# Output projection in half batches of four heads and pairs of query tiles; gates of the expert branch placed by a table

## The chip, the cores and the metric

The kernel runs on one core of a Trainium2 chip. The core has TensorE (matmuls, with weight loads beside them), VectorE, ScalarE, GpSimd and SyncE, which here only issues transfers. Each has its own queue of instructions, worked off in order, and they hand work to each other over semaphores. In the rows PE, PEld, DVE, ACT, POOL and SP stand for TensorE's matmuls, its weight loads, VectorE, ScalarE, GpSimd and SyncE. The metric is the device time of one execution in microseconds (us).

## The reference, cut to what matters

```python
x = L0_attn_x                                # (4, 1024, 256)
xn = _layernorm(x)
# attention: 8 heads of 128, one key and one value for all heads of a batch
q = (xn @ Wq + bq) + pe ; k = (xn @ Wkv + bkv)[..., :128] + pe ; v = ...[..., 128:]
probs = softmax(causal(q k^T / sqrt(128)))
s = concat_over_heads(probs @ v) @ Wo        # (4, 1024, 1024) @ (1024, 256)
# experts: 8 of them, two per token, weighted by the router
f = sum over the token's two experts of gate_e * (relu(xn @ w1_e + b1_e) @ w2_e + b2_e)
out = x + s * silu(f)
```

## The kernel before, in words

Two stages follow each other. Up to about 474 us routing and experts run (`front`); they leave the experts' outputs in DRAM. From then on `attention` runs, and only it is changed.

**Heads and steps.** The four batches have eight heads each, so there are NH = 32 batch-heads, numbered 0 to 31 and called heads here. A head has eight query tiles of 128 rows, done in five groups (`GROUPS`: tile 7; 6 and 0; 5 and 1; 4 and 2; 3). Step k = 5 n + i is group i of head n. Numbers are held as a high and a low half in 16 bits, and each product is three matmuls (`PASSES`).

**A step.** TensorE computes the scores of step k (L1144, L1147 adds the mask) and, one head late, the values of a pair of tiles of head n - 1 (L1167, L1169). VectorE takes row maxima (L1347) from PSUM, ScalarE the exponentials (L1252), VectorE the reciprocals of their sums (L1376), ScalarE the high half of the probabilities (L1282), VectorE the low half (L1383: both of its tensors, `pr` and `ph`, lie in SBUF). SyncE issues a transposing transfer of both halves (L1498), whose result `pT` the values read. The values' result is split into `outs` by ScalarE (L1260) and VectorE (L1389).

**Jobs.** `Jobs` lists one projection of 512 columns for some steps: queries of head n + 2 at i = 0 and 2 of each head, and in heads 4 to 7 of each batch but the last one of keys or values of the next batch at i = 1 (L1101). A query or key job goes TensorE, VectorE (positions, L1356), ScalarE (L1272), VectorE (L1370). The job at i = 0 uses the bank `psJ`, and so does the output projection.

**Output projection before.** `outs` has two buffers of a whole batch. `o_tile(c)` (L1183) multiplies query tile c of a finished batch with `wo` over all eight heads, 24 matmuls of 256 columns into the half bank `psJ[:, 0:D]`. It runs at i = 4 of heads 9 to 31 and once behind the last head, for the TILES = 24 tiles of the first three batches. VectorE multiplies the result by the gate `G` at the start of the next head (`o_gated`, L1410), GpSimd adds `x` (`added`, L1472, 256 columns), SyncE stores and loads 128 KB per tile (L1502, L1507). The last batch's eight tiles are done in `rows_out` (L1194), 192 matmuls of 256 columns in all, into the banks of the scores behind the last head; `closing` (L1443) multiplies them by `G_last` and GpSimd adds `x` (L1487), the last pair VectorE (L1457).

**Gates.** For each of 32 tiles GpSimd fetches the two expert rows of each token (`fetch`, L1466), ScalarE weighs the first (`weigh`, L1290), VectorE adds the second (`whole_f`, L1395), ScalarE takes the tanh (L1301), VectorE forms `G` (`gated`, L1404). Before, one tile is gated in each of heads 1 to 31, at i = 1 to 4, and one behind them: first the last batch's eight, then tiles 0 to 23.

In the loops of all engines i == 0 of the following head comes right behind i == 4; what an engine does there stands first in its step.

## Time and profile before

| | us |
|---|---|
| time, median of three runs (lowest, highest) | 1087.91 (1086.62, 1091.30) |
| the profiled execution: time | 1086.89 |
| its span, first to last instruction | 1085.0 |
| busy: TensorE | 995.2 (92%) |
| busy: VectorE | 859.1 (79%) |
| busy: ScalarE | 644.6 (59%) |
| busy: GpSimd | 324.9 (30%) |

The span is what the profile's clock shows between the first and the last instruction; the time has 1.9 us more around it. Shares are means over stages with different limits, so they are read by stretch. A timeline row gives the start, the duration (of the group, where several like instructions are merged: "x24"), engine, line, operation, and in brackets the idle time of the engine before it with what ended that. A releaser can be misnamed where two events came close together.

### The profile page before, as it was taken

The page shows a single profiled execution, that of the slowest core. Times are in us where ns is not written, and L with a number is a line of the kernel's source. Part 1 is how long each engine was busy: PE and PEld are TensorE (multiplying, and loading weights), DVE is VectorE, ACT ScalarE, POOL GpSimd, SP SyncE. Part 2 cuts the span into 40 slices and gives each one's busy share as a digit, 9 for nine tenths or more (in the row PEclk, how much of TensorE's full clock was granted, in tenths as well). Part 3 has the DMA queues.
Part 4 walks back from the last instruction along what each step waited for, and adds up shares of the span by engine and source line. Part 5 has one row for each costly group of instructions (what it writes and reads, how often), then busy time and mean ns, then how long its engine had stood idle before and what let it go on. Part 6 is the DMA issues. An engine that isn't in the chain of part 4 may idle for free.

```text
span 1085.0 us, 25159 instructions
## 1 busy us (share of the span) xinstructions
PE 995.2 (92%) x8734; PEld 783.7 (72%) x8734; DVE 859.1 (79%) x1543; ACT 644.6 (59%) x1360; POOL 324.9 (30%) x339
## 2 busy tenths in 40 slices
PE   1647999999999999998889889999999999999997
PEld 1536888888888898965656667767677677777776
DVE  6885777666766555569999999998999999999971
ACT  3812333233333333348888888878888888888860
POOL 0005999899994200020011102121112111112111
PEclk9999999999999999999999999999999999999999
DMA  8548776766665312137897888998999879898992
GB/s 281 178 192 182 154 186 172 173 175 178 178 171 157 89 50 55 37 102 147 165 162 141 158 159 177 164 149 153 171 185 178 148 147 170 160 173 160 175 183 90
DMA packets 402810, 168.80 MB, mean 156 GB/s; under 512 B 345562, under 2 KB 393252, under 8 KB 402052
## 3 DMA queue, kind: packets, MB, share of 16 engines
q1 hardware_dynamic: 345632, 127.04, 56.1%
q10 hardware_dynamic: 50580, 22.45, 8.6%
q0 software_dynamic: 6480, 17.70, 6.6%
q8 instruction: 78, 1.28, 0.5%
q14 instruction: 40, 0.33, 0.1%
HBM read 51.66 MB, written 30.67 MB: 76 GB/s over the span
## 4 chain that ended last, share of the span: by engine, by line
PE 35%; DVE 13%; DMA 3%; ACT 3%; issue 2%; SPq 0%; ACTq 0%; DVEq 0%
PE b_psS L1144 10%; PE b_psO L1167 10%; PE b_psJ L1183 5%; PE b_psJ L1101 4%; DVE b_ph L1383 4%; DVE b_nmax L1347 4%; DMA b_pT<-b_ph 3%; PE b_psS L1194 2%; PE b_psS L1101 1%; PE b_psO L1169 1%; DVE b_outs L1389 1%; ACT b_pr L1252 1%; ACT b_ph L1282 1%; DVE b_psJ L1356 1%; PE b_psS L1147 1%
## 5 line engine op out<-in xcount | busy, mean ns | idle before, releaser
L847 PE MATMUL psU<-bxT,w_p 128*128 128x256 f16 (+1 forms) x1920 | 287.9, 263 | 13.3 <-DVE w_p L273 10.4
L922 ACT ACTIVATE h<-psU,bias 128x256 f32<-128x256 f32 (+1 forms) x320 | 124.7, 447 | 284.9 <-PE psU L847 192.8
L856 PE MATMUL psY<-w_p,hp 128*128 x1704 | 272.4, 273 | 1.8 <-DVE hp L944 1.3
L1144 PE MATMUL b_psS<-b_kp,b_Q 128*128 128x512 f16 (+3 forms) x1152 | 218.4, 326 | 0.1
L847 PEld LDWEIGHTS psU<-bxT,w_p 128*128 x1920 | 189.1, 98 | 33.8 <-issue 15.1
L1252 ACT ACTIVATE b_pr<-b_psS,b_nmax 128x1024 f32<-128x1024 f32 (+7 forms) x256 | 186.7, 734 | 42.4 <-DVE b_nmax L1347 22.8
L1167 PE MATMUL b_psO<-b_pT,b_vp 128*128 128x256 f16 x1536 | 188.6, 272 | 18.1 <-issue 8.4
L1383 DVE SCALAR_TENSOR_TENSOR b_ph<-b_pr,b_rrec,b_ph 128x1024 f16<-128x1024 f32 (+7 forms) x256 | 199.1, 809 | 0.0
L1282 ACT ACTIVATE b_ph<-b_pr,b_rrec 128x1024 f16<-128x1024 f32 (+7 forms) x256 | 187.0, 768 | 15.9 <-DVE b_rrec L1376 15.6
L942 DVE CAST hp<-h 128x512 f16<-128x512 f32 (+1 forms) x160 | 88.5, 553 | 134.0 <-ACT h L922 127.1
L1347 DVE TENSOR_REDUCE b_nmax<-b_psS 128x1 f32<-128x1024 f32 (+7 forms) x256 | 182.7, 745 | 9.2 <-PE b_psS L1147 7.3
L856 PEld LDWEIGHTS psY<-w_p,hp 128*128 128x128 f16 x1704 | 166.2, 98 | 22.8 <-issue 2.9
L1167 PEld LDWEIGHTS b_psO<-b_pT,b_vp 128*128 128x128 f16 x1536 | 144.5, 98 | 41.4 <-issue 14.4
L1144 PEld LDWEIGHTS b_psS<-b_kp,b_Q 128*128 128x128 f16 x1152 | 103.0, 98 | 77.2 <-issue 0.6
L1466 POOL DMA_INDIRECT b_yg<-expert_outputs,pos x64 | 68.6, 1071 | 245.0 <-DVE b_f L1395 119.1
L944 DVE TENSOR_TENSOR hp<-h,hp 128x512 f16<-128x512 f32 (+1 forms) x160 | 129.7, 811 | 5.5
L1472 POOL TENSOR_TENSOR b_x_row<-b_G,b_x_row 128x256 f32<-128x256 f32 x24 | 17.4, 726 | 366.9 <-DVE b_G L1410 358.1
L172 POOL DMA_INDIRECT rowx<-xn_split,who x71 | 78.8, 1110 | 99.6 <-DVE who L753 77.2
L1183 PE MATMUL b_psJ<-b_wo,b_outs 128*128 128x256 f16 x576 | 66.9, 273 | 0.3 <-DVE b_Q L1370 0.3
L262 POOL TENSOR_TENSOR w_p<-wstage,w_p 128x512 f16<-128x512 f32 x48 | 64.1, 1336 | 4.1
L1183 PEld LDWEIGHTS b_psJ<-b_wo,b_outs 128*128 128x128 f16 x576 | 55.1, 98 | 7.0 <-DVE b_Q L1370 0.5
L1272 ACT ACTIVATE b_Q<-b_psJ,bias 128x512 f16<-128x512 f32 x59 | 40.5, 687 | 31.3 <-DVE b_psJ L1356 30.6
(181 smaller groups left out, 1029.4 us busy)
## 6 DMA issues: line engine op xcount, KB each, us to landing
wstage<-in_L_ffn_w SPq DMA_DIRECT2D x48, 256.0 KB
expert_rows<-rowx SPq DMA_DIRECT2D x67, 128.0 KB
expert_outputs<-y ACTq DMA_DIRECT2D x31, 256.0 KB
a_x_all<-in_L_attn_x SPq DMA_DIRECT2D x8, 512.0 KB, 9.8
a_w_raw<-in_L_ffn_w SPq DMA_DIRECT2D x4, 1024.0 KB, 6.5
xn_split<-a_xp SPq DMA_DIRECT2D x4, 1024.0 KB, 4.9
xn_turned<-a_xT SPq DMA_DIRECT2D x3, 1024.0 KB, 12.8
b_x_row<-in_L_attn_x SPq DMA_DIRECT2D x24, 128.0 KB, 2.6
```

The costliest lines, as they stand in the source:

```text
L847: mm = eng.matmul(psU[w % U][:, g % 2, 0:tiles * P].rearrange("p (t r) -> p t r", t=tiles), weight(n, a * W1 + c * H + g * P, P), bxT[n % ...
L856: mm = eng.matmul(psY[n % 2][:, t, :], hp[n % 2][:, a, g, t * P:(t + 1) * P], weight(n, 2 * W1 + (2 * g + b) * D, D), start=(g == 0 and k ...
L922: a = eng.activation(h32[w % 4][:, g, 0:rows], psU[w % U][:, g, 0:rows], ACT.Relu, bias=bias[:, ds(e * HT + 2 * q + g, 1)], scale=1.0 / WS)
L942: eng.tensor_copy(hi, full).then_inc(hh_, 1)
L944: eng.tensor_tensor(lo, full, hi, ALU.subtract).then_inc(hl_, 1)
L1144: mm = eng.matmul(dst, Q[n % 3][:, a, u * P:(u + 1) * P], kb[:, c, lo:lo + w], start=(kk == 0), stop=(kk == 2 and not last))
L1167: eng.matmul(both, vb[:, a, j, :], pT[:, at:at + hop + 1:hop, :], start=(j == 0 and kk == 0), stop=False)
L1183: mm = eng.matmul(psJ[:, 0:D], outs[b % many][:, a, h, t * P:(t + 1) * P], wo_p[:, e, h, :], start=(h == 0 and kk == 0), stop=(h == HEADS ...
L1252: a = eng.activation(pr[k % 3][:, o:o + w], psS[BUF[i]][:, :, :].rearrange("p a n -> p (a n)")[:, o:o + w], ACT.Exp, bias=nmax[:, at:at + ...
L1282: a = eng.activation(ph[k % 4][:, 2 * o:2 * o + w], pr[k % 3][:, o:o + w], ACT.Copy, scale=rrec[:, at:at + 1])
L1347: a = eng.tensor_reduce(nmax[:, at:at + 1], psS[BUF[i]][:, :, :].rearrange("p a n -> p (a n)")[:, o:o + w], AX.X, ALU.max, negate=True)
L1383: a = eng.scalar_tensor_tensor(ph[k % 4][:, 2 * o + w:2 * o + 2 * w], pr[k % 3][:, o:o + w], rrec[:, at:at + 1], ph[k % 4][:, 2 * o:2 * o ...
```

## The change

The output projection works on half batches. `outs` is one buffer of a batch. Portion r (`o_pair(r)`, r = 0 to 27) takes four heads (the first or the second half of a batch's eight) and two query tiles: 2 x 4 x 3 = 24 matmuls of 256 columns, into the whole bank `psJ`. It runs at i = 4 of head r + 5, that is of heads 5 to 31, and portion 27 behind the last head. `two_of(r)` gives which half it is and the number g of the pair of tiles.

- First half of the heads (r % 8 below 4): ScalarE copies the bank to `part` (`o_part`), at the start of heads 6 to 9, 14 to 17, 22 to 25, 30, 31 and behind them.
- Second half: VectorE adds the bank to `part` (`o_sum`), at the start of heads 10 to 13, 18 to 21 and 26 to 29; then GpSimd multiplies `part` by `G` (`weighted`) and adds it to `x_rows` (`added`), each 512 columns; SyncE loads and stores pairs of 256 KB.
- Last batch: its first four heads are portions 24 to 27. GpSimd multiplies them by `G_last` and adds them to `x_last` (`added_last`), which is loaded (1 MB) in head 8 and no longer behind the last head. `rows_out` keeps heads 4 to 7: 96 matmuls.
- Gates follow the table `gates`: tiles 0 to 23 in heads 4 to 27, the last eight as a second gate, one step later, in heads 12 to 15 and 20 to 23. Heads 1 to 3 and 28 to 31 have none.
- New waits: ScalarE waits for the experts' stores ahead of its loop, VectorE for four `added_last` ahead of the last head's `o_low`.

```diff
-    seq = list(range(TILES, NT)) + list(range(TILES))
-    turn_of = {c: s for s, c in enumerate(seq)}
+    PART, MORE = HEADS // 2, TILES // 2
+    gates = [(5 * n + 1 + x, c) for n in range(NH) for x, c in enumerate(
+        ([n - PART] if PART <= n < PART + TILES else []) + ([TILES + n % HEADS - PART + n // HEADS * PART - PART]
+                                                            if n % HEADS >= PART and 0 < n // HEADS < 3 else []))]
+    gate_at = dict(gates)
+    turn_of = {c: s for s, (_, c) in enumerate(gates)}
...
-        xr = [sb(f"x_row{i}", [P, D], F32) for i in range(3)]
+        xr = [sb(f"x_rows{i}", [P, 2, D], F32) for i in range(3)]
...
-        Gb = [sb(f"G{i}", [P, D], F32) for i in range(2)]
-        outs = [sb(f"outs{i}", [P, 2, HEADS, T], F16) for i in range(2)]
+        Gp = [sb(f"G{i}", [P, 2, D], F32) for i in range(4)]
+        part = [sb(f"part{i}", [P, 2, D], F32) for i in range(4)]
+        outs = sb("outs", [P, 2, HEADS, T], F16)
...
-        over = Arena(nc, q_at)
-        fin = over.take("b_x_last", [P, QT, D], F32)
...
+        def two_of(r):
+
+            m, p = r // 4, r % 4
+            return m % 2, 4 * (m // 2) + p
+
+        def bank_free(eng, r):
+
+            second, g = two_of(r)
+            eng.wait_ge(ot_ if second else oe_, g + 1)
...
-            def o_tile(c):
...
+            def o_pair(r):
+
+                m, p = r // 4, r % 4
...
-                eng.wait_ge(al_, 2 * HEADS * (b + 1))
-                if c:
-                    eng.wait_ge(ot_, c)
-                for h in range(HEADS):
-                    for kk, (a, e) in enumerate(PASSES):
-                        mm = eng.matmul(psJ[:, 0:D], outs[b % many][:, a, h, t * P:(t + 1) * P], wo_p[:, e, h, :],
-                                        start=(h == 0 and kk == 0), stop=(h == HEADS - 1 and kk == 2))
+                eng.wait_ge(al_, 2 * PART * (m + 1))
+                if r:
+                    bank_free(eng, r - 1)
+                h0 = PART * (m % 2)
+                for x in range(2):
+                    t = 2 * p + x
+                    for h in range(h0, h0 + PART):
+                        for kk, (a, e) in enumerate(PASSES):
+                            mm = eng.matmul(psJ[:, x * D:(x + 1) * D], outs[:, a, h, t * P:(t + 1) * P], wo_p[:, e, h, :],
+                                            start=(x == 0 and h == h0 and kk == 0), stop=(x == 1 and h == h0 + PART - 1 and kk == 2))
                 mm.then_inc(om_, 1)
...
-                        if i == 0 and n >= HEADS + 2:
-                            eng.wait_ge(ot_, n - HEADS - 1)
+                        if i == 0 and n >= PART + 2:
+                            bank_free(eng, n - PART - 2)
...
-                    if i == 4 and n > HEADS:
+                    if i == 4 and n > PART:
                         eng.wait_ge(jl_, jobs.issued(k + 1))
-                        o_tile(n - HEADS - 1)
+                        o_pair(n - PART - 1)
...
-            rows_out(0, 0, HEADS - 2)
-            o_tile(TILES - 1)
+            rows_out(0, PART, HEADS - 2)
+            o_pair(NH - PART - 1)
...
             rows_out(0, HEADS - 2, HEADS - 1)
-            rows_out(3, 0, HEADS - 1)
+            rows_out(3, PART, HEADS - 1)
...
-            rows_out(2, 0, HEADS - 1)
...
-            rows_out(1, 0, HEADS - 1)
+            rows_out(1, PART, HEADS - 1)
...
-                if n >= 2 * HEADS and n % HEADS == 0 and half == 0:
-                    eng.wait_ge(om_, n - HEADS)
+                if n >= HEADS and n % PART == 0 and half == 0:
+                    eng.wait_ge(om_, n - PART)
...
+            def o_part(g):
+                eng.wait_ge(om_, 4 * (2 * (g // 4)) + g % 4 + 1)
+                if g >= 4:
+                    eng.wait_ge(oa_, g - 3)
+                eng.activation(part[g % 4][:, :, :].rearrange("p t d -> p (t d)"), psJ[:, :], ACT.Copy, scale=0.5 / WS).then_inc(oe_, 1)
...
+            for i, o in enumerate(v["y_o"]):
+                eng.wait_ge(o, 16 * len(range(i, NBLK, 3)))
             for k in range(LAST + 2):
                 n, i = k // 5, k % 5
+                if i == 0 and n >= PART + 2 and not two_of(n - PART - 2)[0]:
+                    o_part(two_of(n - PART - 2)[1])
...
-                if k < LAST and n:
-                    if i == 1:
-                        weigh(seq[n - 1])
-                    if i == 3:
-                        tanh(seq[n - 1])
-            weigh(TILES - 1)
-            tanh(TILES - 1)
+                if k in gate_at:
+                    weigh(gate_at[k])
+                if k - 2 in gate_at:
+                    tanh(gate_at[k - 2])
+            o_part(two_of(NH - PART - 1)[1])
...
-                if 2 <= c < TILES:
-                    eng.wait_ge(oa_, c - 1)
-                dst = Gb[c % 2][:, :] if c < TILES else GD[:, c - TILES, :]
+                if 8 <= c < TILES:
+                    eng.wait_ge(oa_, c // 2 - 3)
+                dst = Gp[c // 2 % 4][:, c % 2, :] if c < TILES else GD[:, c - TILES, :]
...
-            def o_gated(c):
-                g = Gb[c % 2][:, :]
-                eng.wait_ge(G_, turn_of[c] + 1)
-                eng.wait_ge(om_, c + 1)
-                eng.scalar_tensor_tensor(g, psJ[:, 0:D], 0.5 / WS, g, ALU.mult, ALU.mult).then_inc(ot_, 1)
+            def o_sum(g):
+                whole = part[g % 4][:, :, :].rearrange("p t d -> p (t d)")
+                eng.wait_ge(oe_, g + 1)
+                eng.wait_ge(om_, 4 * (2 * (g // 4) + 1) + g % 4 + 1)
+                eng.scalar_tensor_tensor(whole, psJ[:, :], 0.5 / WS, whole, ALU.mult, ALU.add).then_inc(ot_, 1)
...
-                if i == 0 and n >= HEADS + 2:
-                    o_gated(n - HEADS - 2)
+                if i == 0 and n >= PART + 2 and two_of(n - PART - 2)[0]:
+                    o_sum(two_of(n - PART - 2)[1])
...
-                if k < LAST and n:
-                    if i == 2:
-                        whole_f(seq[n - 1])
-                    if i == 4:
-                        gated(seq[n - 1])
+                if k - 1 in gate_at:
+                    whole_f(gate_at[k - 1])
+                if k - 3 in gate_at:
+                    gated(gate_at[k - 3])
...
-            whole_f(TILES - 1)
-            gated(TILES - 1)
-            o_gated(TILES - 1)
+            eng.wait_ge(fe_, 4)
...
-            def added(c):
-                eng.wait_ge(ot_, c + 1)
-                eng.wait_ge(xq[c % 3], 16 * (c // 3 + 1))
-                eng.tensor_tensor(xr[c % 3][:, :], Gb[c % 2][:, :], xr[c % 3][:, :], ALU.add).then_inc(oa_, 1)
+            def flat(t):
+                return t.rearrange("p t d -> p (t d)")
+
+            def weighted(g):
+                eng.wait_ge(G_, max(turn_of[2 * g], turn_of[2 * g + 1]) + 1)
+                eng.tensor_tensor(flat(part[g % 4][:, :, :]), flat(part[g % 4][:, :, :]), flat(G_of(g)), ALU.mult).then_inc(og_, 1)
+                eng.wait_ge(og_, g + 1)
+
+            def added(g):
+                eng.wait_ge(ot_, g + 1)
+                weighted(g)
+                eng.wait_ge(xq[g % 3], 16 * (g // 3 + 1))
+                eng.tensor_tensor(flat(xr[g % 3][:, :, :]), flat(part[g % 4][:, :, :]), flat(xr[g % 3][:, :, :]), ALU.add).then_inc(oa_, 1)
+
+            def added_last(g):
+                eng.wait_ge(oe_, g + 1)
+                weighted(g)
+                eng.wait_ge(xf_, 16)
+                j = g - MORE
+                eng.tensor_tensor(flat(fin[:, 2 * j:2 * j + 2, :]), flat(part[g % 4][:, :, :]), flat(fin[:, 2 * j:2 * j + 2, :]), ALU.add).then_inc(fe_, 1)
...
-                if i == 1 and n >= HEADS + 2:
-                    added(n - HEADS - 2)
-                if i == 3 and n < NH:
-                    fetch(seq[n])
-            added(TILES - 1)
-            eng.wait_ge(xf_, 16)
+                if i == 1 and n >= PART + 2:
+                    second, g = two_of(n - PART - 2)
+                    if second:
+                        added(g)
+                    elif g >= MORE:
+                        added_last(g)
+                if k + 3 in gate_at:
+                    fetch(gate_at[k + 3])
+            added_last(MORE + 3)
...
-                eng.dma_start(of[:, c, :], xr[c % 3][:, :]).then_inc(xo[c % 3], 16)
+                eng.dma_start(of[:, 2 * c:2 * c + 2, :], xr[c % 3][:, :, :]).then_inc(xo[c % 3], 16)
 
             def inputs(c):
                 if c >= 3:
                     eng.wait_ge(xo[c % 3], 16 * (c // 3))
-                eng.dma_start(xr[c % 3][:, :], xf[:, c, :]).then_inc(xq[c % 3], 16)
+                eng.dma_start(xr[c % 3][:, :, :], xf[:, 2 * c:2 * c + 2, :]).then_inc(xq[c % 3], 16)
 
             eng.wait_ge(v["wk_"], 64)
             eng.dma_start(wo_p[:, :, :, :], v["wo_d"]).then_inc(wol, 16)
@@ -1514,14 +1558,12 @@
                 n, i = k // 5, k % 5
                 if k >= 2:
                     turn(k - 2)
-                if i == 1 and n >= HEADS + 1:
-                    inputs(n - HEADS - 1)
-                if i == 3 and n >= HEADS + 2:
-                    stored(n - HEADS - 2)
-            eng.wait_ge(sc_, LAST)
-            eng.dma_start(fin[:, :, :], xf[:, TILES:, :]).then_inc(xf_, 16)
-            for c in (TILES - 2, TILES - 1):
-                stored(c)
```

TensorE, behind the last head (`b_psS` is the closing rows' target, `b_psJ` the portion's; `b_psO` rows are the last head's values). Before:

```order
L1183 MATMUL b_psJ<-b_wo,b_outs_22522 128x256 x24
L1194 MATMUL b_psS<-b_wo,b_outs_22523 128x256 x36
L1183 MATMUL b_psJ<-b_wo,b_outs_22522 128x256 x24
L1194 MATMUL b_psS<-b_wo,b_outs_22523 128x256 x48
L1167 MATMUL b_psO<-b_pT,b_vp_22500 128x256 x21
L1169 MATMUL b_psO<-b_pT,b_vp_22500 128x128 x3
L1167 MATMUL b_psO<-b_pT,b_vp_22500 128x256 x3
L1169 MATMUL b_psO<-b_pT,b_vp_22500 128x128 x3
L1194 MATMUL b_psS<-b_wo,b_outs_22523 128x256 x54
```

The same place after:

```order
L1204 MATMUL b_psJ<-b_wo,b_outs 128x256 x24
L1214 MATMUL b_psS<-b_wo,b_outs 128x256 x12
L1204 MATMUL b_psJ<-b_wo,b_outs 128x256 x24
L1214 MATMUL b_psS<-b_wo,b_outs 128x256 x24
L1185 MATMUL b_psO<-b_pT,b_vp_22500 128x256 x21
L1187 MATMUL b_psO<-b_pT,b_vp_22500 128x128 x3
L1185 MATMUL b_psO<-b_pT,b_vp_22500 128x256 x3
L1187 MATMUL b_psO<-b_pT,b_vp_22500 128x128 x3
L1214 MATMUL b_psS<-b_wo,b_outs 128x256 x30
```

Of the closing rows 36, 48, 54 and (further on) 54 have become 12, 24, 30 and 30; the order around them is the same.

VectorE, at the start of a head with a second half (`b_ph`, `b_pr` are the probabilities of L1383, which is L1411 after). Before:

```order
L1404 SCALAR_TENSOR_TENSOR b_G_22520<-b_th_22518,b_f_22516 128x256
L1410 SCALAR_TENSOR_TENSOR b_G_22520<-b_psJ,b_G_22520 128x256
L1376 RECIPROCAL b_rrec<-b_rsum 128x1
L1389 SCALAR_TENSOR_TENSOR b_outs_22522<-b_psO,bias,b_outs_22522 128x512
L1347 TENSOR_REDUCE b_nmax<-b_psS 128x1
L1383 SCALAR_TENSOR_TENSOR b_ph_22509<-b_pr_22526,b_rrec,b_ph_22509 128x640
L1383 SCALAR_TENSOR_TENSOR b_ph_22509<-b_pr_22526,b_rrec,b_ph_22509 128x384
L1356 SCALAR_TENSOR_TENSOR b_psJ<-b_psJ,pe_sb 128x512
```

After:

```order
L1432 SCALAR_TENSOR_TENSOR b_G_22522<-b_th_22519,b_f_22517 128x256
L1438 SCALAR_TENSOR_TENSOR b_part_22524<-b_psJ,b_part_22524 128x512
L1404 RECIPROCAL b_rrec<-b_rsum 128x1
L1417 SCALAR_TENSOR_TENSOR b_outs<-b_psO,bias,b_outs 128x512
L1375 TENSOR_REDUCE b_nmax<-b_psS 128x1
L1411 SCALAR_TENSOR_TENSOR b_ph_22509<-b_pr_22531,b_rrec,b_ph_22509 128x640
L1411 SCALAR_TENSOR_TENSOR b_ph_22509<-b_pr_22531,b_rrec,b_ph_22509 128x384
L1384 SCALAR_TENSOR_TENSOR b_psJ<-b_psJ,pe_sb 128x512
```

The step on the bank of the projection keeps its place, adds instead of multiplying, and has 512 columns for 256.

GpSimd, between the fetches (L1466 before, L1491 after) of two heads with second halves. Both, as the difference has it:

```order
-L1472 TENSOR_TENSOR b_x_row_22501<-b_G_22520,b_x_row_22501 128x256
-L1466 DMA b_yg_22514<-expert_outputs,pos 128x256 x2
-L1472 TENSOR_TENSOR b_x_row_22502<-b_G_22521,b_x_row_22502 128x256
+L1499 TENSOR_TENSOR b_part_22524<-b_part_22524,b_G_22520 128x512
+L1506 TENSOR_TENSOR b_x_rows_22501<-b_part_22524,b_x_rows_22501 128x512
+L1491 DMA b_yg_22514<-expert_outputs,pos 128x256 x2
+L1499 TENSOR_TENSOR b_part_22525<-b_part_22525,b_G_22521 128x512
+L1506 TENSOR_TENSOR b_x_rows_22502<-b_part_22525,b_x_rows_22502 128x512
```

One step of 256 columns in each head has become two of 512 columns, all operands in SBUF, in twelve heads; in the other heads of the loop GpSimd has fetches alone until head 30.

## Rows read from the trace of the kernel before

**Rows 1.** Busy time by stretch: bounds, length, engines (instructions), PEclk, DMA share, GB/s

```profile
core 0: us, PE busy (x) PEld busy (x) DVE busy (x) ACT busy (x) POOL busy (x), PEclk, DMA share, GB/s
499.71:551.04 51.33, 45.21 (x355) 31.14 (x354) 48.67 (x88) 43.90 (x91) 5.67 (x6) 1.00 0.91 173
551.04:622.36 71.32, 65.25 (x527) 45.06 (x526) 68.69 (x123) 60.67 (x125) 7.55 (x8) 1.00 0.80 147
785.99:820.83 34.84, 34.84 (x282) 25.23 (x280) 33.37 (x61) 29.72 (x61) 6.14 (x6) 1.00 0.92 178
838.55:914.79 76.24, 76.24 (x623) 54.33 (x622) 70.21 (x127) 61.77 (x124) 11.91 (x12) 1.00 0.85 152
```

**Rows 2.** Timeline, ScalarE: first exponential of head 18 (start, us, what, idle before)

```profile
803.41 1.11 ACT L1252 ACTIVATE b_pr<-b_psS,b_nmax 128x1024 f32<-128x1024 f32 x1 [1.11 <-issue]
```

**Rows 3.** Timeline, TensorE: first values matmuls behind the seams of heads 5 to 9

```profile
586.42 0.81 PE L1167 MATMUL b_psO<-b_pT,b_vp 128*128 128x256 f16 x6 [1.48 <-DVE b_outs L1389]
...
604.34 0.92 PE L1167 MATMUL b_psO<-b_pT,b_vp 128*128 128x256 f16 x7 [1.63 <-issue]
...
622.09 1.14 PE L1167 MATMUL b_psO<-b_pT,b_vp 128*128 128x256 f16 x9 [1.45 <-DVE b_outs L1389]
...
639.48 0.71 PE L1167 MATMUL b_psO<-b_pT,b_vp 128*128 128x256 f16 x5 [2.43 <-DMA b_pT<-b_ph]
```

**Rows 4.** Timeline, TensorE: from the last portion but one to the closing rows

```profile
1045.81 2.78 PE L1183 MATMUL b_psJ<-b_wo,b_outs 128*128 128x256 f16 x24
1048.43 4.09 PE L1194 MATMUL b_psS<-b_wo,b_outs 128*128 128x256 f16 x36
...
1060.22 2.46 PE L1167 MATMUL b_psO<-b_pT,b_vp 128*128 128x256 f16 x21
...
1063.17 6.06 PE L1194 MATMUL b_psS<-b_wo,b_outs 128*128 128x256 f16 x54
```

**Rows 5.** Timeline, VectorE and GpSimd: start of head 18

```profile
801.04 0.42 DVE L1410 SCALAR_TENSOR_TENSOR b_G<-b_psJ,b_G 128x256 f32<-128x256 f32 x1
801.55 0.73 POOL L1472 TENSOR_TENSOR b_x_row<-b_G,b_x_row 128x256 f32<-128x256 f32 x1 [13.98 <-DVE b_G L1410]
803.29 1.40 DVE L1383 SCALAR_TENSOR_TENSOR b_ph<-b_pr,b_rrec,b_ph 128x640 f16<-128x640 f32 x2
808.43 0.17 DVE L1376 RECIPROCAL b_rrec<-b_rsum 128x2 f32<-128x2 f32 x1 [0.56 <-ACT b_pr L1252]
```

**Rows 6.** Expert stage: two timeline rows, and L944 by line (ns min/median/max)

```profile
182.88 1.21 POOL L262 TENSOR_TENSOR w_p<-wstage,w_p 128x512 f16<-128x512 f32 x1
183.10 1.53 DVE L944 TENSOR_TENSOR hp<-h,hp 128x512 f16<-128x512 f32 x1
...
L944 DVE TENSOR_TENSOR hp<-h,hp x160: 424/693/1531, 91.7 to 469.5; 128x512 f16<-128x512 f32 x124, 128x256 f16<-128x256 f32 x36
```

**Rows 7.** Groups by line: busy us, mean ns of one, idle before

```profile
L1395 DVE SCALAR_TENSOR_TENSOR b_f<-b_yg,gate,b_f 128x256 f32<-128x256 f32 x32 | 15.3, 478 | 0.0
L1410 DVE SCALAR_TENSOR_TENSOR b_G<-b_psJ,b_G 128x256 f32<-128x256 f32 x24 | 10.2, 425 | 4.2 <-PE b_psJ L1183 3.5
L1443 DVE SCALAR_TENSOR_TENSOR b_G_last<-b_psS,b_G_last 128x512 f32<-128x512 f32 x4 | 2.7, 692 | 7.5 <-PE b_psS L1194 7.5
L1487 POOL TENSOR_TENSOR b_x_last<-b_G_last,b_x_last 128x512 f32<-128x512 f32 x3 | 3.8, 1265 | 16.1 <-DVE b_G_last L1443 16.1
```

**Rows 8.** Transfers: a chain piece, GpSimd's first fetch, two TensorE waits, last transposes issued

```profile
507.30 5.59 DMA b_pT<-b_ph
...
474.09 0.94 POOL L1466 DMA_INDIRECT b_yg<-expert_outputs,pos  x1 [112.36 <-DMA expert_outputs<-y]
...
776.91 1.80 PE L1167 MATMUL b_psO<-b_pT,b_vp 128*128 128x256 f16 x15 [0.86 <-issue]
...
1042.15 1.80 PE L1167 MATMUL b_psO<-b_pT,b_vp 128*128 128x256 f16 x15 [1.02 <-issue]
...
1049.31 6.90 SPq L1498 DMA_TRANSPOSE b_pT<-b_ph  x3
```

28 lines of the change are left out of this document (18 added, 10 removed).

## Prediction

> **What bounds the kernel now.** I read the busy time by stretch first, because the change touches the attention stage alone (474 us to the end) and the page's shares average over three different limits. The stretches of [rows 1] run from the first exponential of one head to that of another; head 18's is shown [rows 2]. Heads 1 to 3 take 51.33 / 3 = 17.11 us each, with TensorE idle 6.1 us of the 51.3 and VectorE idle only 2.7: VectorE, with one hand-over to ScalarE and back, sets the pace. Heads 4 to 7 take 17.83 each, TensorE idle 6.07 of 71.32: the same limit, with key and value jobs on top. Heads 17 and 18 take 17.42 with TensorE busy 34.84 of 34.84, and heads 20 to 23 take 19.06 with TensorE full: there TensorE is the bound, and the output projection (L1183, one query tile per head from head nine on) is what filled it. The granted clock is 1.00 in all of them.
>
> Second, the TensorE timeline at the heads' seams. Before the first values of a batch-head it waits 1.48, 1.63, 1.45 and 2.43 us at the seams of heads 5/6, 6/7, 7/8 and 8/9 [rows 3]; behind head nine these holes are closed. Third, the end: from 1048.43 TensorE runs 192 projection matmuls of the last batch, the 24 of the last tile and 54 + 54 of closing rows, with no hole before 1060.22 [rows 4]. So the tail is TensorE work in a line, and each matmul less there is time.
>
> **The change, part by part.**
>
> *Work moved from the tail into heads 5 to 8.* A query tile over eight heads has 24 matmuls, and so has a pair of tiles over four heads. Before there are 24 such portions and 192 matmuls of closing rows; after, 28 portions and 96 of closing rows: the sum is the same 768. A portion takes 1048.43 - 1045.81 = 2.62 us, 0.109 per matmul [rows 4]. The tail loses 96 x 0.109 = **-10.5**. Four portions are new in heads 5 to 8 and bring 4 x 2.62 = 10.5, of which 1.48 + 1.63 + 1.45 + 2.43 = 6.99 fall into the holes: **+3.5**. Is the shorter tail held by something else? TensorE would come to the first values (1060.22 before) 48 matmuls earlier, at 1055.0, and to the third at 1055.0 + 2.95 + 30 x 0.109 = 1061.2. The last three transposes are issued up to 1056.2, and one takes up to 5.59 us to land [rows 4, 8]: about 1060. VectorE's new wait for four added pairs stands ahead of the last head's low half: the last portion ends at 1052.4, ScalarE's copy and GpSimd's 2 x 1.27 [rows 7] end near 1055.7, and VectorE is wanted at 1055.0 + 2.95 + 0.7 = 1058.7. Both are covered, by 1 and 3 us; without cover either costs what it is late.
>
> *Gates moved.* Heads 1 to 3 lose theirs: two steps of 256 columns on VectorE, 0.48 the first [rows 7] (0.40 start to start), and the second, which falls where VectorE waits for ScalarE anyway; I take 0.4 a head, **-1.2** (bounds 0 and -2.7). Heads 28 to 31 lose theirs too. TensorE is full in 28 and 29 and waits in 31 (1.02 at 1042.15 [rows 8]) and a little in 29 and 30: **-1.0** (0 to -2). Heads 12 to 15 and 20 to 23 get a second gate, 2 x 0.4 = +0.8 on VectorE and as much on ScalarE, which waits more; VectorE is idle 76.24 - 70.21 = 6.0 there, 1.5 a head [rows 1].
>
> *Output halves.* In heads 6 to 9, 14 to 17, 22 to 25 and 30, 31 ScalarE copies a pair out (512 columns) and VectorE does nothing for it, 0.42 less than before. ScalarE waits 1.11 ahead of the head's first exponential [rows 2], and the copy is shorter: nothing. In heads 10 to 13, 18 to 21 and 26 to 29 VectorE adds 512 columns instead of multiplying 256: 0.692 - 0.425 = +0.27 [rows 7].
>
> *GpSimd.* This decides. Before it adds 256 columns in each head, 0.73 us, right behind L1410, beside a high-low split that reads PSUM and a maximum: nothing is stretched [rows 5]. After, in the twelve heads of second halves, it multiplies 512 columns and then adds 512 columns, 1.27 each [rows 7]. Count from the end S of VectorE's new sum: multiply S + 0.1 to S + 1.36, add S + 1.45 to S + 2.7. VectorE's next two-operand step, the low halves L1383, starts 803.29 - 801.46 = 1.83 behind L1410's end [rows 5], so at S + 1.83, in the middle of the add. What such an overlap costs has a row of the expert stage: the GpSimd product 182.88 to 184.09, and VectorE's subtraction of two SBUF tensors from 183.10 takes 1.53, where the median is 0.693 [rows 6]. It ends 0.54 behind GpSimd, 0.15 less than it takes alone. So L1383 ends 0.15 sooner than add plus itself: 2.7 - 1.83 - 0.15 = **0.72 later**, and behind it stand the position step, ScalarE's query copy and the whole head.
>
> The Trainium skill ("SBUF — State Buffer", Who interferes with whom) says that a VectorE instruction with two SBUF inputs and a GpSimd instruction that reads SBUF take a port in turns, the later one fully blocked. The rows of the expert stage agree; the attention stage of this kernel shows no such meeting, since its GpSimd step lies beside other instructions. By its neighbours in the stage the new pair would cost 0, by the rule and the row above 0.72 a head.
>
> Now per head of second halves, against TensorE's need. Heads 10, 11, 18, 19, 26, 27: VectorE busy 33.37 / 2 = 16.69, + 0.56 that it waits for ScalarE in every head [rows 5], + 0.27 + 0.72 = 18.24 against 17.42: +0.82, six times 4.9. Heads 28, 29: less a gate, 17.44: 0. Heads 12, 13, 20, 21: busy 17.55, and 0.3 more for the position step of key jobs, + 0.8 gate + 0.27 + 0.72 + 0.4 (the least idle time of such a head, from [rows 1]: 2.6 in four heads) = 20.0 against 19.1: +0.85, four times 3.4. TensorE's lead over VectorE swallows the first 0.7 of each of three runs: 8.3 - 2.1 = **+6.2** (bounds 0, if nothing is blocked, and 8.3).
>
> *Transfers.* 24 loads and 24 stores of 128 KB become 12 and 12 of 256 KB in the same queue as the transposes, and 1 MB goes from the tail into head 8. Transposes behind them come later; the longest wait that shows it is 0.86 (776.91 [rows 8]), and half the heads lose theirs: +0.5 (0 to 5). ScalarE's new wait for the expert stores costs 0: GpSimd's wait for the same ended at 474.09 [rows 8], and ScalarE's next step is the first exponential, some ten us later.
>
> **The sum**, against the profiled execution (1086.89, span 1085.0; the median of the three timed runs is 1087.91): -10.5 + 3.5 - 1.2 - 1.0 + 6.2 + 0.5 = -2.5, so **1084.4**.
>
> **The rivals.** *The low halves are not blocked* (GpSimd's pair runs elsewhere or the two do not meet). For it: not one of the 24 meetings in this stage stretches anything [rows 5]. Against: they meet other instructions. Then 6.2 becomes 0 and the time is 1078.2. *Half of it*: VectorE's delay is partly taken by waits that it has anyway; 3.1 less, 1081.3. *Slower than before*: the doubled transfers. If every one of the 24 holds a transpose long enough that TensorE waits 0.43, half of the longest row, it is 24 x 0.43 = 10.3: 1094.7. It turns slower from 0.15 a transfer on; for it, landings close to their use at L1167, against, that half of the heads have none. *It does not do what it says*: the holes of rows 3 are not filled but move (the portion sits ahead of the next head's scores, on which VectorE waits). Then +7.0: 1091.4.
>
> **How the numbers follow.** Forecast 0.48; not blocked 0.20; half 0.15; transfers 0.09; holes move 0.08. A measurement of this kernel tells about 0.5% from no change: below 1082.5 is faster, above 1093.3 slower. Faster takes the two cheap rivals (half is near the bound, so two thirds of it) and the low edge of the forecast: 0.34. Slower takes the transfers: 0.09. Range: from the unblocked case to the moved holes, 1078 to 1091.
>
> **What would show it.** Right: TensorE full from head 6 on in first-half heads, tail shorter by 10 us, heads 1 to 3 at 16.7; heads 10, 11, 18, 19 at 18.2 with TensorE holes of 0.8, and the low halves of 640 columns at 1.6 us instead of 0.88 beside the second GpSimd instruction. Wrong: these at 0.88 and the heads at 17.4 (first rival); landings of transposes late at L1167 (transfers); holes at the seams of heads 5 to 8 as before.

## The result and the profile after

The changed kernel takes **1091.41 us** (median of 20 runs, 1088.58 to 1103.35); the kernel before, run beside it, takes 1086.16 (20 runs, 1081.54 to 1095.01). The ratio is 1.0048, with a 95% interval of 1.0026 to 1.0070: slower, by 2.8 to 7.6 us. The forecast was 1084.4, with a range up to 1091. So the sign was wrong, and the time lies 0.4 us above the upper end of the range. The profiled execution has a span of 1089.88 against 1085.03 before, 4.85 more.

The first view is again the busy time by stretch, from one head's first exponential to another's. The stretches are heads 1 to 3, 4 to 7, 10 and 11, 14 and 15, and 20 to 23; the columns are those of [rows 1].

```profile
core 0: us, PE busy (x) PEld busy (x) DVE busy (x) ACT busy (x) POOL busy (x), PEclk, DMA share, GB/s
496.09:548.62 52.53, 48.54 (x359) 32.72 (x358) 47.32 (x82) 42.03 (x84) 0.00 (x0) 0.95 0.84 154
548.62:623.70 75.08, 71.75 (x586) 50.98 (x586) 68.89 (x123) 62.47 (x128) 7.55 (x8) 1.00 0.78 140
658.72:694.76 36.04, 35.30 (x282) 25.21 (x281) 34.91 (x61) 29.49 (x61) 11.65 (x11) 1.00 0.96 192
733.79:773.98 40.19, 38.01 (x329) 27.85 (x328) 35.29 (x65) 32.96 (x68) 7.56 (x8) 1.00 0.80 151
846.65:925.95 79.30, 75.49 (x619) 53.95 (x618) 73.45 (x131) 65.32 (x135) 21.25 (x21) 1.00 0.80 155
```

TensorE, full in heads 20 to 23 before [rows 1], now waits 3.8 us in them, and 2.2 in heads 14 and 15. Head by head, from the first exponentials of both profiles, the 4.85 us come from here:

| stretch | before | after | measured | forecast |
|---|---|---|---|---|
| start to head 0 (not touched) | 483.97 | 480.34 | -3.63 | 0 |
| heads 1 to 3 | 51.33 | 52.53 | +1.20 | -1.2 |
| heads 5 to 8 | 70.50 | 74.64 | +4.14 | +3.5 |
| head 9 | 17.14 | 17.51 | +0.37 | 0 |
| heads 10 to 13, 18 to 21, 26, 27 | 181.52 | 187.63 | +6.11 | +6.7 |
| heads 14, 15, 22, 23 | 75.98 | 80.32 | +4.34 | 0 |
| heads 16, 17, 24, 25 | 70.04 | 70.64 | +0.60 | 0 |
| heads 28 to 31 | 64.40 | 66.45 | +2.05 | -1.0 |
| last exponential to the end | 36.50 | 26.12 | -10.38 | -10.5 |

(Head 31 is counted to the end of its last exponential.) Heads 0 and 4 are within 0.1 of before. The two large terms of the sum, the tail and the second-half heads, came out as worked out. What sank the forecast most is the row of heads 14, 15, 22 and 23, which I had put at nothing; heads 28 to 31 come second, 3.05 us from their forecast.

**The tail.** TensorE's timeline from the last portion of the step loop to the closing rows, which answers to [rows 4] (start, us, what, number of matmuls, idle time before):

```profile
1060.01 2.78 PE L1204 MATMUL b_psJ<-b_wo,b_outs 128*128 128x256 f16 x24
1062.63 1.47 PE L1214 MATMUL b_psS<-b_wo,b_outs 128*128 128x256 f16 x12
1065.07 2.78 PE L1204 MATMUL b_psJ<-b_wo,b_outs 128*128 128x256 f16 x24 [0.96 <-ACT b_part L1322]
1067.68 2.78 PE L1214 MATMUL b_psS<-b_wo,b_outs 128*128 128x256 f16 x24
1070.30 2.46 PE L1185 MATMUL b_psO<-b_pT,b_vp 128*128 128x256 f16 x21
...
1073.26 3.44 PE L1214 MATMUL b_psS<-b_wo,b_outs 128*128 128x256 f16 x30
```

The closing blocks have 12, 24 and 30 matmuls where [rows 4] has 36 and 54, and nothing new is late at the first values (1070.30), apart from 0.96 us for ScalarE's copy of the bank.

**The lock.** By this I mean that GpSimd's pair and VectorE's low halves, when they meet, do not run at the same time. VectorE and GpSimd at the start of head 11, which answers to [rows 5]:

```profile
674.16 0.69 DVE L1438 SCALAR_TENSOR_TENSOR b_part<-b_psJ,b_part 128x512 f32<-128x512 f32 x1
...
676.61 2.14 DVE L1411 SCALAR_TENSOR_TENSOR b_ph<-b_pr,b_rrec,b_ph 128x640 f16<-128x640 f32 x2
...
674.93 1.27 POOL L1499 TENSOR_TENSOR b_part<-b_part,b_G 128x512 f32<-128x512 f32 x1 [12.61 <-DVE b_part L1438]
676.28 1.26 POOL L1506 TENSOR_TENSOR b_x_rows<-b_part,b_x_rows 128x512 f32<-128x512 f32 x1
```

The pair of low halves (L1411) takes 2.14 here and 1.40 in [rows 5]; its 640-column part alone takes 1.61 instead of 0.88. It is so in all twelve second-half heads: 1.60 to 1.62 in eleven of them, 1.44 in head 29. That part ends at 678.22, 0.68 behind the end of GpSimd's add; the forecast was 0.72 later than alone, and it is 0.73. In heads 30 and 31 the same pair takes 2.44 and 2.36 beside GpSimd's add of the last tiles (L1513), which was not in my sum.

**The seams.** The holes of [rows 3] are filled, not moved; what is left behind them is a wait of 0.39 at the first job of heads 6, 7 and 8. The first and the last of the three:

```profile
583.61 1.46 PE L1119 MATMUL b_psJ<-b_xTb_other,wq_late 128*128 128x512 f16 x6 [0.39 <-issue]
...
622.33 1.46 PE L1119 MATMUL b_psJ<-b_xTb_other,wq_late 128*128 128x512 f16 x6 [0.39 <-issue]
```

Between heads 14 and 15, of two gates each, the same wait is 1.09. TensorE, ScalarE and VectorE there:

```profile
747.56 2.79 PE L1204 MATMUL b_psJ<-b_wo,b_outs 128*128 128x256 f16 x24
...
752.80 1.46 PE L1119 MATMUL b_psJ<-xTb_next,wq_late 128*128 128x512 f16 x6 [1.09 <-issue]
...
749.33 1.33 ACT L1302 ACTIVATE b_ph<-b_pr,b_rrec 128x640 f16<-128x640 f32 x2 [0.70 <-DVE b_rrec L1404]
...
751.24 0.67 ACT L1280 ACTIVATE b_outs<-b_psO,bias 128x512 f16<-128x512 f32 x1
751.80 0.41 ACT L1327 ACTIVATE b_th<-b_f 128x256 f32<-128x256 f32 x1
752.11 0.59 ACT L1322 ACTIVATE b_part<-b_psJ 128x512 f32<-128x512 f32 x1
...
748.74 0.48 DVE L1423 SCALAR_TENSOR_TENSOR b_f<-b_yg,gate,b_f 128x256 f32<-128x256 f32 x1
```

The portion is done at 750.35. Its bank (psJ) is wanted for the query job as soon as the scores behind the portion are done, at 751.71, but ScalarE copies it out only at 752.11 to 752.70. The second gate's step on VectorE (L1423, 0.48) delays the reciprocal that ScalarE waits for (0.70, where it is 0.30 with one gate), and the second gate's tanh (L1327 at 751.80) puts the copy off by another 0.31. Both are ahead of the bank's release, so TensorE, the bound of these heads, pays for them.

### The profile page after: what moved, and what is told of

It is laid out like the page before. It is cut to its first block, busy times and chain, and to the rows that moved or that the text cites. A ratio compares the mean times of both kernels' runs of the same rounds, so it can differ in the third digit from the quotient of the medians.

```text
span 1089.9 us, 25159 instructions
## 1 busy us (share of the span) xinstructions
PE 998.1 (92%) x8734; PEld 783.4 (72%) x8734; DVE 869.6 (80%) x1531; ACT 651.1 (60%) x1376; POOL 343.1 (31%) x347
## 4 chain that ended last, share of the span: by engine, by line
PE 36%; DVE 13%; ACT 4%; issue 3%; DMA 1%; SPq 0%; ACTq 0%; DVEq 0%
PE b_psS L1162 11%; PE b_psO L1185 11%; PE b_psJ L1204 5%; PE b_psJ L1119 5%; DVE b_ph L1411 4%; DVE b_nmax L1375 4%; ACT b_pr L1272 2%; PE b_psS L1119 2%; DVE b_outs L1417 1%; PE b_psO L1187 1%; ACT b_ph L1302 1%; PE b_psS L1165 1%; DVE b_psJ L1384 1%; PE b_psS L1214 1%; DVE b_Q L1398 1%
## 5 line engine op out<-in xcount | busy, mean ns | idle before, releaser
L1411 DVE SCALAR_TENSOR_TENSOR b_ph<-b_pr,b_rrec,b_ph 128x1024 f16<-128x1024 f32 (+7 forms) x256 | 212.2, 861 | 0.0
L942 DVE CAST hp<-h 128x512 f16<-128x512 f32 (+1 forms) x160 | 91.2, 570 | 131.9 <-ACT h L922 131.5
L1491 POOL DMA_INDIRECT b_yg<-expert_outputs,pos x64 | 64.5, 1008 | 352.2 <-DVE b_f L1423 225.2
L944 DVE TENSOR_TENSOR hp<-h,hp 128x512 f16<-128x512 f32 (+1 forms) x160 | 125.4, 784 | 5.5
L1499 POOL TENSOR_TENSOR b_part<-b_part,b_G 128x512 f32<-128x512 f32 x12 | 15.2, 1270 | 211.9 <-DVE b_part L1438 211.9
L1204 PE MATMUL b_psJ<-b_wo,b_outs 128*128 128x256 f16 x672 | 78.1, 273 | 1.2 <-ACT b_part L1322 1.0
L1204 PEld LDWEIGHTS b_psJ<-b_wo,b_outs 128*128 128x128 f16 x672 | 63.9, 98 | 10.0 <-issue 1.2
```

The source lines that it names most:

```text
L942: eng.tensor_copy(hi, full).then_inc(hh_, 1)
L944: eng.tensor_tensor(lo, full, hi, ALU.subtract).then_inc(hl_, 1)
L1204: mm = eng.matmul(psJ[:, x * D:(x + 1) * D], outs[:, a, h, t * P:(t + 1) * P], wo_p[:, e, h, :], start=(x == 0 and h == h0 and kk == 0), s ...
L1411: a = eng.scalar_tensor_tensor(ph[k % 4][:, 2 * o + w:2 * o + 2 * w], pr[k % 3][:, o:o + w], rrec[:, at:at + 1], ph[k % 4][:, 2 * o:2 * o ...
```

## The experiments

Theory A: the loss is the lock in second-half heads plus the second gate in the key and value heads. Rival B: the 256 KB transfers of residual rows hold the transposes. Rival C: something that belongs to neither edit (the clock, the untouched stage).

### Lock and gates, alone and together

The changed kernel was run again beside the three, so that all four share a chip.

> The changed kernel again, as a control beside the others. Theory A (GpSimd's pair blocks the low halves, and the second gate makes ScalarE's copy late at the seams of heads 12 to 15 and 20 to 23) and theory B (larger transfers in the transposes' queue, and other things of the run) both expect about 1091.4. Asked beside: whether the attention stage again starts some 3.6 us sooner than in the kernel before, whether the granted clock again falls to 0.5 for 3.4 us in heads 1 and 3, and whether TensorE again waits 2.04 us in head 19. If these come back they belong to the kernel, if not to the run.

Measured: 1093.48, ratio 1.0060 (1.0041 to 1.0079), span 1091.7. Of the three side questions: the stage starts early again (480.13), there are again stretches at a granted clock of 0.5 (1.2 GHz), but one of the two lies elsewhere (the first in heads 0 and 1, the second now in head 5, which takes 20.10), and TensorE waits only 1.31 us in head 19 this time.

**GpSimd's pair narrowed**, the two adds like the product below, so most of the output is left out and the time is a price (what the work left out costs), not that of a usable kernel:

```
-  eng.tensor_tensor(flat(part[g % 4][:, :, :]), flat(part[g % 4][:, :, :]), flat(G_of(g)), ALU.mult)
+  eng.tensor_tensor(flat(part[g % 4][:, :, :])[:, 0:8], flat(part[g % 4][:, :, :])[:, 0:8], flat(G_of(g))[:, 0:8], ALU.mult)
```

> Leaves out work: GpSimd multiplies and adds 8 of 512 columns of each pair (so most of the gated sum is not formed), all waits and transfers stay. Theory A: the low halves of 640 columns fall from 1.61 to 0.88 us, heads 10, 11, 18, 19, 26 and 27 from 18.0 to 17.5, heads 12, 13, 20, 21 by 0.4 to 0.7, heads 30 and 31 by 0.7 each, while heads 14, 15, 22, 23 stay at 20.1: together -5 to -7, about 1085.5. Theory B: GpSimd's pair costs nothing beside VectorE's wait, the time stays within 1 us of 1091.4.

Measured: 1087.59, ratio 1.0012 (0.9991 to 1.0033), 5.9 below the run of the changed kernel.

**One gate per head**, all the work in it:

```
-    gates = [(5 * n + 1 + x, c) for n in range(NH) for x, c in enumerate(
-        ([n - PART] if PART <= n < PART + TILES else []) + ([TILES + n % HEADS - PART + n // HEADS * PART - PART]
-                                                            if n % HEADS >= PART and 0 < n // HEADS < 3 else []))]
+    gates = [(3, TILES)] + [(5 * n + 1, n - PART if PART <= n < PART + TILES else TILES + n - (TILES if n >= PART else 0))
+                            for n in range(1, NH)]
```

> One gate per head: the last batch's eight tiles are gated in heads 0 to 3 and 28 to 31, no head has two. Theory A: heads 14, 15, 22, 23 fall from 20.07 to about 19.1 us and TensorE's wait of 1.09 at their seams to the 0.39 of heads 6 and 7; heads 12, 13, 20, 21 fall by 0.4; heads 0 to 3 and 28 to 31 lose at most 0.4 each: together -4 to -6, about 1086.5. Theory B (the wait at the seams is ScalarE's copy of the half batch alone, with the gate beside the point): 20.07 stays, time 1091 to 1093.

Measured: 1088.26, ratio 1.0024 (1.0002 to 1.0045), 5.2 below. ScalarE and TensorE at the end of head 14 here, where the profile of the changed kernel has 0.70 and 1.09:

```profile
749.10 1.34 ACT L1301 ACTIVATE b_ph<-b_pr,b_rrec 128x640 f16<-128x640 f32 x2 [0.30 <-DVE b_rrec L1403]
...
751.57 0.59 ACT L1321 ACTIVATE b_part<-b_psJ 128x512 f32<-128x512 f32 x1
...
752.26 1.46 PE L1118 MATMUL b_psJ<-xTb_next,wq_late 128*128 128x512 f16 x6 [0.39 <-issue]
```

**Both:**

> Both: one gate per head, and GpSimd's pair of 8 columns (work left out as in the narrow run). Theory A: the two gains add, -9 to -12, about 1081, 5 us below the kernel before, since then TensorE is the bound from head 5 on and the tail is 10 us shorter. Theory B: transfers keep TensorE waiting, 1087 or more. If both mechanisms hide one another the sum is less than the two apart.

Measured: **1078.85**, ratio 0.9932 (0.9908 to 0.9955), 14.6 below. By heads, in us from first exponential to first exponential:

| heads | before | after | narrow pair | one gate | both |
|---|---|---|---|---|---|
| 10 | 17.14 | 18.02 | 17.41 | 18.02 | 17.42 |
| 20 | 19.31 | 19.81 | 19.81 | 19.42 | 19.41 |
| 21 | 18.99 | 19.36 | 19.36 | 18.96 | 18.96 |
| 22 | 18.98 | 20.07 | 20.06 | 19.37 | 19.37 |

The table separates the prices. In head 10 it is the lock alone (0.61 of 0.88; the other 0.27 brings it to the 17.42 at which TensorE is full in heads 17 and 18 [rows 1]). In heads 20 and 21 it is the gate alone: with two gates the lock costs nothing more. (In heads 12 and 13 together neither edit alone gains anything, 39.04 after, 39.17 and 39.23, and both together gain 0.7, 38.34; which of the two binds there is not separated.) In heads 14, 15, 22, 23 it is the gate, 0.70 each, and 0.39 remains with one gate. VectorE and GpSimd of the run with both, at the start of head 11:

```profile
674.87 1.41 DVE L1410 SCALAR_TENSOR_TENSOR b_ph<-b_pr,b_rrec,b_ph 128x640 f16<-128x640 f32 x2
...
673.47 0.20 POOL L1505 TENSOR_TENSOR b_x_rows<-b_part,b_x_rows 128x8 f32<-128x8 f32 x1
```

Theory A stands for the two prices. The two prices together (14.6) are more than one by one (5.9 + 5.2). Part of the difference is not explained by the heads above: the profile of the run with both starts its attention stage 1.6 to 1.8 us sooner than that of the changed kernel beside it and than the one with the narrow pair (478.56 against 480.13 and 480.30), and its head 30 takes 15.84 against 16.90 to 17.32 in the others. The last does not belong to the two edits: a later run that has both of them and one more takes 17.45 in head 30. So some of the 14.6 may be chance.

### The transfers

Loads and stores of residual rows cut to 8 columns, the loads from the fourth on like the store below:

```
-  eng.dma_start(of[:, 2 * c:2 * c + 2, :], xr[c % 3][:, :, :])
+  eng.dma_start(of[:, 2 * c:2 * c + 2, 0:8], xr[c % 3][:, :, 0:8])
```

> The changed kernel, whose loads and stores of residual rows (256 KB each, twelve and twelve) carry 8 columns instead of 256, but for the first three loads; most of the output rows are left out, so its time is a price and no version. Transfer theory: the transpose in front of head 19's wait lands in 4 to 5 us instead of 8.06, that wait (1.3 to 2.0) goes, head 11's and head 30's too, and the time is 3 to 5 below the changed kernel: 1087 to 1089. If the holes come from the lock and the second gate alone (they were still 0.5 to 0.8 without these), heads 19 and 30 keep 1 us or more and the time is 1090 to 1092.

Measured: 1090.94, ratio 1.0042 (1.0029 to 1.0055), 2.5 below the second run of the changed kernel and 0.5 below the first; its interval overlaps with both, so the times alone do not show a gain. Head 19 is where it shows. Its TensorE wait was 2.04 in the changed kernel's first profile, behind three transposes in SyncE's queue. SyncE and TensorE of that profile, then TensorE with the small transfers:

```profile
825.59 8.94 SPq L1542 DMA_TRANSPOSE b_pT<-b_ph  x3
...
837.53 1.80 PE L1185 MATMUL b_psO<-b_pT,b_vp 128*128 128x256 f16 x15 [2.04 <-DVE b_outs L1417]
```

```profile
835.23 1.80 PE L1185 MATMUL b_psO<-b_pT,b_vp 128*128 128x256 f16 x15 [0.70 <-issue]
```

(The releaser named in the first is long done; the transpose of group 3 landed at 837.43, 8.06 us behind its issue.) That is 1.3 us in one head of twelve against the first profile and 0.6 against the second, where the wait is 1.31. Head 11 (TensorE waits 0.67 against 0.60 and 0.71) and head 30 (1.82 in all against 2.00 and 2.22) keep their holes. Rival B is worth about a microsecond at most in what the heads show. The second half of my expectation, that heads 11 and 30 owe theirs to these transfers, fell.

### The copy of the bank

Where the 0.39 us comes from that is left in first-half heads with key or value jobs: first with ScalarE's copy narrowed, on top of the run with both edits (its work left out from head 14 on, so a price).

```
-  eng.activation(part[g % 4][:, :, :].rearrange("p t d -> p (t d)"), psJ[:, :], ACT.Copy, scale=0.5 / WS)
+  eng.activation(part[g % 4][:, :, :].rearrange("p t d -> p (t d)")[:, 0:(8 if g >= 4 else 512)], psJ[:, 0:(8 if g >= 4 else 512)], ACT.Copy, scale=0.5 / WS)
```

> The run with one gate per head and GpSimd's narrow pair, in which from the fifth pair on (heads 14 to 17, 22 to 25, 30, 31) ScalarE's copy of the first half carries 8 columns instead of 512; that part of the output is left out, so its time is a price. If the 0.39 us that TensorE still waits at the start of heads 14, 15, 22, 23 is the length of ScalarE's copy (0.59), the wait goes and these heads take 19.0 instead of 19.37, the heads 16, 17, 24, 25 17.42 instead of 17.51: 1.5 to 2 us less in all. If the wait is the hand-over and ScalarE's order, it stays above 0.3 and the time is the same as without this edit.

Measured: 1078.41, ratio 0.9913 (0.9896 to 0.9931) against 0.9932 without the edit. The medians tell the two apart no better than that; the heads do. TensorE and ScalarE at the end of head 14, where the job is at once behind the scores now:

```profile
751.88 0.22 PE L1164 MATMUL b_psS<-maskb,idb 128*128 128x128 bf16 x1
752.08 1.45 PE L1118 MATMUL b_psJ<-xTb_next,wq_late 128*128 128x512 f16 x6
...
751.80 0.17 ACT L1321 ACTIVATE b_part<-b_psJ 128x8 f32<-128x8 f32 x1
```

Heads 15, 22 and 23 take 18.95, 18.95 and 18.94 instead of 19.37, heads 16 and 24 17.12 and 17.11 instead of 17.50 and 17.51, and the wait is gone. In heads 6 and 7, where the copy is not narrowed, they stay at 19.36 and 19.37. The copy is 0.42 us shorter (0.17 for 0.59) and each of the three heads is too, although the engine that makes it waits 0.85 a step later in the run with both edits: what was cut off it came back in full. (Its span, 1079.6, is not below the 1076.9 of that run: its attention stage starts 3.56 later, and its head 30 takes 1.61 more.)

Then the copy moved ahead of the second high half, with all the work in it (on the held-back version below):

```
-                if i == 0 and n >= PART + 2 and not two_of(n - PART - 2)[0]:
-                    o_part(two_of(n - PART - 2)[1])
...
                     expo(k)
+                    if i == 4 and PART < n and not two_of(n - PART - 1)[0]:
+                        o_part(two_of(n - PART - 1)[1])
                     if n and i in (2, 4):
```

> The same as the run before it, with one more edit: in first-half heads ScalarE copies the output bank out ahead of the second high half of the attention output, and no longer as the first step of the next head. If TensorE's wait of 0.39 us ahead of the key, value or query job at the start of heads 6 to 9, 14 to 17, 22 to 25 comes from ScalarE's order, it goes in heads 6, 7, 14, 15, 22, 23 (19.37 to 19.0) and the time falls by 2 to 3 us against that run. If the copy then holds up the high half, the values of the next head wait instead and nothing or the other way is gained: 0 to +3.

Measured: 1087.21, ratio 1.0009 (0.9986 to 1.0032), against 1085.07 of the held-back version beside it; their intervals overlap. Heads 6 and 7 fall from 19.37 to 18.82 and 18.81 as the first theory says, but heads 5, 13 and 21, in which the copy now stands ahead of the high half, rise by 0.53, 0.49 and 0.49. Heads 5 to 8 together gain 0.5 of the 1.1. The greater part of the price is passed on.

### A version with the pair out of the way

Held back: one gate per head, as above, and GpSimd's pair moves from i = 1 to i = 4 of its loop, behind the fetch, and waits until VectorE has finished the head's position step (or, in heads without a second job, the low halves). It then lies beside a maximum and steps that read PSUM. All the work is in it. The core of the edit:

```
+            def window(n):
+                if 5 * n + 2 in jobs.at:
+                    eng.wait_ge(jp_, jobs.turned(jobs.at[5 * n + 2]))
+                else:
+                    eng.wait_ge(lo_, 5 * n + 1)
             def added(g, n):
                 eng.wait_ge(ot_, g + 1)
+                window(n)
```

> All the work of the changed kernel, with two edits: one gate per head (the last eight tiles gated in heads 0 to 3 and 28 to 31), and GpSimd's pair of 512-column steps held back until VectorE is past the position step, so that it lies beside steps that read no two tensors of SBUF. Lock theory: the low halves of 640 columns are back at 0.88 us, heads 10, 11, 26, 27 at 17.4, heads 12, 13, 20, 21 near 19.0 to 19.3, as with the narrow pair, and the time is 1079 to 1081, below the kernel before. If what the narrow pair saved was GpSimd's time itself (the residual rows that it delivers late), the gain is not there: 1086 to 1088. If the pair meets other two-tensor steps instead (the whole of a gate's input, or the low halves of the next group): heads 10, 11 at 18.0 again, 1086.

Measured: 1085.07, ratio 0.9994 (0.9975 to 1.0013). Short of the 1079 to 1081 expected. The lock part holds. VectorE's low halves in head 11, with GpSimd's full 512-column pair in the kernel:

```profile
673.02 1.40 DVE L1410 SCALAR_TENSOR_TENSOR b_ph<-b_pr,b_rrec,b_ph 128x640 f16<-128x640 f32 x2
```

Heads 10, 11, 26 and 27 take 17.50, 17.40, 17.49 and 17.42. But TensorE waits 2.74 at head 14, 1.65 at head 22 and 2.26 at head 30, each the first head after a run of second halves. The first two are new. The third is not: head 30 has 2.00 in the changed kernel and 2.16 with one gate. SyncE, TensorE and GpSimd at the first:

```profile
727.38 0.57 SPq L1555 DMA_DIRECT2D out<-b_x_rows  x1
728.05 13.17 SPq L1551 DMA_TRANSPOSE b_pT<-b_ph  x4
...
738.41 0.49 PE L1184 MATMUL b_psO<-b_pT,b_vp 128*128 128x256 f16 x3 [2.74 <-DMA b_pT<-b_ph]
...
723.26 1.67 POOL L1490 DMA_INDIRECT b_yg<-expert_outputs,pos  x1
725.23 1.50 POOL L1490 DMA_INDIRECT b_yg<-expert_outputs,pos  x1 [0.30 <-issue]
727.04 0.95 POOL L1490 DMA_INDIRECT b_yg<-expert_outputs,pos  x1 [0.30 <-issue]
728.29 0.95 POOL L1490 DMA_INDIRECT b_yg<-expert_outputs,pos  x1 [0.30 <-issue]
```

The hold kept GpSimd's fetches one tile behind; when the run of pairs ends, two tiles are fetched within 6 us, and the transpose issued at 728.05 takes 10.23 us to land. (Head 14's 23.43 holds a short fall of the clock as well; in the run with the copy moved, which has a like wait, 3.13, and none of that, it is 21.77.) The mend is to pass the same point in every head:

```
+                if i == 4 and 0 < n < PART + 2:
+                    window(n)
                 if (i == 4 or k == LAST + 2) and n >= PART + 2:
                     second, g = two_of(n - PART - 2)
+                    if not second and g < MORE:
+                        window(n)
```

> The held-back pair with one gate per head, all the work in it, and one more edit: GpSimd passes the same waiting point in every head, also where it has no pair. In the run without this edit GpSimd's fetches of expert rows are one behind in second-half heads, and the first head after each run of them (14, 22, 30) has two tiles' fetches (2 x 2 DMAs) within 6 us, beside a store of 256 KB and the transposes; a transpose lands after 10.23 us and TensorE waits 2.74, 1.65 and 2.26 us there. If the two fetches together are the cause, head 14 comes back to 19.4, head 22 to 19.4 and head 30 to 15.9, and the time falls by 5 to 6 us to 1079, below the kernel before. If the store is the cause, or the held-back pair itself, the waits stay and the time is 1085.

Measured: **1083.70**, ratio 0.9977 (0.9960 to 0.9994) to the kernel before. Short of the 1079 expected. Heads 14 and 22 come back to 19.36 and 19.37, and there is one tile per head:

```profile
737.75 0.49 PE L1184 MATMUL b_psO<-b_pT,b_vp 128*128 128x256 f16 x3
...
742.30 0.94 POOL L1490 DMA_INDIRECT b_yg<-expert_outputs,pos  x1 [13.34 <-DVE b_psJ L1383]
743.54 0.95 POOL L1490 DMA_INDIRECT b_yg<-expert_outputs,pos  x1 [0.30 <-issue]
```

Head 30 does not come back (18.98, with 2.16 of waits on TensorE and a short fall of the clock; 17.82 before the mend, with 2.26 of waits). So the piled-up fetches were the cause in heads 14 and 22, and not in head 30; what holds that one stays open. This version, with all the work and one gate per head, is faster than both kernels, by 0.1 to 0.4% against the one before and, by the two ratios (each to the kernel before on its own chip), by 0.7% against the changed one.

### The kernel before as a control

In the first profile of before, no stretch of the attention stage up to the last head was at the lower clock; in the changed kernel's, two short ones were. And the stage began 3.63 us earlier, behind code that the change leaves alone. Three more profiles of before:

> The kernel before, once more, as a second profile of it. If the short stretches at the lower granted clock in heads 0 to 5, and the start of the attention stage some 4 us earlier, belong to the changed kernel, then this profile has neither: heads 1 and 3 at 17.11, first exponential at 484. If they are chance, it may have one of them: a head of 0 to 5 that is 0.8 to 2 us longer than in the first profile. Time 1086, as before.

> The kernel before once more, for the part of it that the change does not touch. If the expert stage's end is later in it as such, the first exponential comes at 484 or later again, as in its two profiles, and short stretches at the lower granted clock may fall anywhere in heads 0 to 5. If the two late starts were chance, it comes near 480, as in the nine profiles of the changed kernel and its variants.

> The same once more: a second look at the start of the attention stage of the kernel before, 484 to 487 if it is the kernel's, near 480 if it is chance.

Measured: 1084.97 median of 9 runs for the first (ratio 0.9993, 0.9973 to 1.0012; its profiled span 1092.0), and single runs of 1088.31 and 1087.68. The first exponentials come at 486.62, 481.13 and 480.76, so the start varies by itself, from 480.8 to 486.6 in four profiles of before and from 478.5 to 482.1 in ten of the changed kernel and its versions. All three have stretches at the lower clock in heads 0 to 4, the last one another at 637.7: head 1 takes 18.98, 17.98 and 18.00 there instead of 17.11, head 4 19.61, 19.60 and 17.94 instead of 17.92. In all three the loop from first to last exponential takes 568.5 to 568.9, where the first profile has 564.56. Rival C is thus right about the profiles and wrong about the kernels: the lower clock belongs to neither. Against the controls the changed kernel's loop (583.42) is 14.5 to 14.9 longer, and the tail 10.4 shorter: +4.1 to +4.5, next to the 5.25 between the medians.

## Why the prediction was wrong, point by point

**Tail, right.** -10.38 against -10.5.

**Heads 5 to 8, nearly right.** +4.14 against +3.5. The portions fill the holes of [rows 3] as said, and the rival of the moving holes fell. But the sum had TensorE full there, and it still waits 1.54 us (three times 0.39, and 0.37 of a wait that begins in head 4), so that the row is only 0.6 over is in part luck. Head 5 takes 18.40 here and 17.89 with one gate per head, for which I have no cause.

**Lock, right in the price; its sum is in part luck.** 0.73 for the block against 0.72, heads 10, 11, 26, 27 at 18.02 against 18.24. The Trainium skill ("SBUF — State Buffer", Who interferes with whom) says that such a meeting blocks the later instruction fully. The trace agrees but for 0.2 us: the low half ends 0.68 behind GpSimd's add, and had it waited to the add's end it would end 0.88 behind. The row of the expert stage, from which the 0.72 came, falls short of a full wait in the same way, by 0.15. The sum of +6.11 for ten heads against +6.7 is less good than it looks. Heads 10, 11, 18, 19, 26 and 27 gave +4.5 of the 4.9 that I had for them ahead of TensorE's lead, and the narrow pair gives 3.9 of it back (3.2 against the second profile of the changed kernel, the difference being head 19). Heads 12, 13, 20 and 21 gave +1.6 for 3.4, and there the narrow pair gives back nothing: in 20 and 21 the loss is the second gate's. The term of these four heads was also added up wrongly: the least idle time of [rows 1] is 2.63 us in four heads, 0.66 a head and not 0.4, and even with 0.4 the terms give 20.04 against 19.06, +0.98 and not +0.85.

**The second gate: the step that failed.** I had written that heads 12 to 15 and 20 to 23 get +0.8 on VectorE "and as much on ScalarE, which waits more", with VectorE idle 1.5 a head, and took the idle time as cover; in heads 14, 15, 22, 23 nothing of it entered the sum. It costs 0.70 a head there (20.07 against 19.37 with one gate), and 0.30 in each of heads 16 and 24 behind them (17.81 against 17.51). By the trace the 0.70 are 0.40 of the longer wait for the reciprocal and 0.31 of the tanh; no run takes the two apart. An engine's idle time says whether it has room in the head, not whether the room lies ahead of the hand-over that TensorE waits for. The room was behind it: VectorE idles while ScalarE takes the exponentials; the gate's steps fall between the last scores and the release of the bank.

**The copy at "nothing": the second part of it.** I had argued that ScalarE waits 1.11 ahead of the first exponential [rows 2] and so could take the copy. It has the time, and the copy is on the path all the same: TensorE is at the bank's next job at 751.7 and ScalarE's copy comes behind a high half. It costs about 0.4 in each of heads 14, 15, 22, 23, 16 and 24: shown by the narrowed copy. Heads 6 and 7 have the same wait of 0.39, which goes when the copy is moved. Before, VectorE took the same bank out with 256 columns at the first place in its line (801.04 [rows 5]) and TensorE waited nowhere for it. In heads 14, 15, 22 and 23 the two, 0.70 and 0.39 each, make 4.36 of the +4.34 where the sum had 0; they are also in the +0.60 of heads 16, 17, 24 and 25. Head 9's +0.37 belongs to neither as far as the runs show: TensorE has no wait in it, and heads 17 and 25, which stand where head 9 does, keep 17.48 with the narrowed copy.

**Gates gone from heads 1 to 3: -1.2 forecast, nothing found.** Head 2, the one undisturbed in both, takes 17.06 against 17.11. In the run with the small transfers, where the clock holds, all three heads take 17.06, and in the held-back version, where they have one gate each, 17.11 or 17.12. VectorE is busy 47.32 in the three heads instead of 48.67 and idle for the difference. I read these heads as a chain of hand-overs between ScalarE and VectorE in whose slack the two steps lay; that reading is not shown by a run of its own. This is the same error as above, the other way round: VectorE at 95% busy was taken for the bound. The +1.20 of the table is the clock, at 0.95 in that stretch; before's own controls lie at 52.21 to 53.22 there.

**Heads 28 to 31: -1.0 forecast, +2.05 measured.** The lock in heads 30 and 31, which I had not put there, accounts for part (head 31 takes 13.16 with the narrow pair and 14.05 without). TensorE's waits in head 30, 2.00 in all, are two: 0.81 at scores that follow ScalarE's exponentials, and 1.18 at values. Before they are 0.62. With the narrow pair the first is gone and the second 1.92. They come to 1.8 to 2.3 in every other version but the run with both edits, where they are 0.66, and they are 2.30 again in the run that adds the narrowed copy to it. Neither the residual transfers nor the fetches nor the lock nor the second gate explains them, and I leave it open.

**Transfers: +0.5 forecast,** +0.6 to +1.3 in head 19, nothing clear elsewhere. The rival with 10.3 fell.

**The start of the stage, 3.63 earlier,** is scatter between executions for the most part: two profiles of before start at 480.8 and 481.1, inside the range of the changed ones. Four profiles of before do not rule out that some of it is the kernel's. Without it the sum of the profile differences would have been +8.5; I compared with a profile that was lucky in the loop (4 us below its controls) and unlucky in the stage ahead of it.

The mechanism of each of the two large terms was right. The cause of the wrong sign is two terms set at zero by counting idle time: without their 4.34 in heads 14, 15, 22 and 23 the 4.85 would be 0.5, and the +4.1 to +4.5 against the controls about nothing. Heads 28 to 31, 3.05 off, are the second part of the miss and are only half explained.

## What to carry to other kernels

Ask of each added step what it stands ahead of in its engine's order, and who waits for that; an engine that idles 1.5 us a head can still delay the bound engine by the whole length of a step, if its idle time lies behind the hand-over. A bank that changes hands between the bound engine and a helper is worth a row of its own in the sum: once the bound engine has work for the bank and waits, each part of the copy that is still to come is a loss. And when a queue's work is held back, look at the point where the hold ends: what had piled up comes at once, beside the transfers of that moment.

## What the runs showed of the hardware

TensorE's granted clock fell to 0.5 for a few us within the first six heads in eleven of the fourteen profiles, not in the first one of before. Four have such a stretch later in the loop. The first control of the kernel before, TensorE ahead of and behind an idle time of 3.42, and then the windows of its heads 1 and 2:

```profile
492.93 1.46 PE L1101 MATMUL b_psJ<-xTb_next,wq_late 128*128 128x512 f16 x6
...
499.87 2.74 PE L1101 MATMUL b_psJ<-xTb_next,wq_late 128*128 128x512 f16 x6 [3.42 <-DVE b_Q L1370]
```

```profile
502.36:521.34 18.98, 17.86 (x128) 11.74 (x126) 16.42 (x30) 14.87 (x30) 1.89 (x2) 0.92 0.81 160
521.34:538.46 17.12, 15.06 (x117) 10.40 (x118) 16.23 (x30) 14.64 (x30) 1.89 (x2) 1.00 0.88 173
```

The same six matmuls take 1.46 at 2.4 GHz and 2.74 at 1.2, and head 1 is 1.87 longer than in the first profile. Such a stretch costs a head up to 2 us (head 1 of the changed kernel's second profile, 19.11) and comes and goes between executions of the same program, which is about the size of what this change did.

The lock works both ways. In head 30 of the changed kernel VectorE's low halves begin 0.07 ahead of GpSimd's add. The first keeps its 0.88, the add takes 1.95 instead of 1.27, and the second low half, which then comes behind the add, 1.65 instead of 0.60. Both halves in one row:

```profile
1032.62 2.44 DVE L1411 SCALAR_TENSOR_TENSOR b_ph<-b_pr,b_rrec,b_ph 128x640 f16<-128x640 f32 x2
...
1032.69 1.95 POOL L1513 TENSOR_TENSOR b_x_last<-b_part,b_x_last 128x512 f32<-128x512 f32 x1
```
